# Gate logits kept in their PSUM bank, and the layer norm's epsilon added by a two-operand instruction, in a fused cross-attention and gated self-attention kernel

## The chip, the cores and the metric

The kernel runs on one core of one Trainium2 chip. The metric is the device time of one execution in microseconds; the time before is the median of three runs. A second number, the span, is the stretch of one profiled execution from its first to its last instruction.

## What is computed

Eight sequences of 1024 tokens, 512 channels wide, go through two residual blocks. The first is cross-attention to a context of 1024 by 384 (8 heads of 64), the second self-attention (16 heads of 32) whose output is scaled, token by token, by gates. All is fp32.

```
x = x + tanh(g_xattn) * attn1(layernorm(x), ctx)
x = x + tanh(g_ffn)   * attn2(layernorm(x))

layernorm(x) = (x - mean) / sqrt(var + 1e-5)

# in attn2, per token, on the attention's output h:
gates  = softmax(h @ Wr.T + br)            # 15 routed
routed = gates * top3_mask * 3
sw     = softmax(h @ Ws.T + bs)            # 2 shared
shared = 2 * sw[0] * sw
routed = 2 * sw[1] * routed
out    = h * (shared.sum() + routed.sum())
return out @ Wp.T + bp
```

## The kernel before

The program is one long software pipeline over 16 units called batches here: 0 to 7 are the cross-attention of the eight sequences, 8 to 15 the self-attention of the same eight. Each batch has four groups of heads, each group 16 steps T (two halves of the queries by eight tiles of keys). A step computes scores on TensorE (item `S`, line 920), their exponentials on ScalarE (`ex`, L1122, written to a ring of SBUF buffers), and the weighted values on TensorE (`PV`, L937). The softmax's sums are made on GpSimd, which adds exponential buffers onto one another (`ad`, L812: 128x512, both operands and the result in SBUF, a run of 24 of them per eight steps in the self-attention) before a matmul with ones (`sm`, L949). While one group is attended, the next is projected (`pq`, `pk`, L834), the row maxima of its scores are taken (`mx` on TensorE, L897, and `mxr` on VectorE, L1275), and the next batch is loaded and normed.

A class `Plan` lists every item with its engine, a guessed time, a due step and what it must come after, and simulates the five queues; `Order` turns the result into one fixed order per engine, into semaphore counts, and into the PSUM bank of each unit. The guessed time decides order and banks, not correctness. PSUM's eight banks are one for the weighted values, three for scores, and a ring of four, `aux`, for everything else. A unit holds its bank until the instruction that Order calls its taker counts up `emptied`; the next unit of that bank waits for the count (`wait_emptied`). For the gates' logits the unit is `gt` and the taker `gm`. Every engine works through its list strictly in order.

Two places matter here.

The layer norm of a half batch (items `ln`, `la`, `lb`, `l2`): VectorE takes statistics (L1220, L1223), adds epsilon to four variances (L1225), ScalarE takes logarithm and exponential of them (`la`, L1022 and L1023), VectorE does one Newton step and the bias (`lb`: L1229, L1172, L1173, L1232; all their operands lie in SBUF), and ScalarE norms four tiles (`l2`, L1030), which TensorE transposes (`tr`, L854). There are 32 such halves, named `(batch, half)`.

The gates of a half batch (item `gm`, 16 of them, two per self-attention batch): four tiles of 18 logits lie in one bank of `aux` (L958). VectorE adds the bias and writes the sums to SBUF (L1308), which releases the bank. Everything after works in SBUF: maxima (L1312, L1313), subtractions (L1314, L1315), ScalarE's exponential (L1155), top values and sums (L1318 to L1322), and eight small instructions of 128x4 that combine them into `sc`, the factor per token (L1324 to L1332). `link` marks an instruction whose result the next one reads: VectorE waits for it on its own semaphore. The outputs' evacuation (`ope`, L1340) reads `sc`.

## Time and profile before

| what | us |
|---|---|
| median of 3 runs (5220.41 to 5243.31) | 5229.36 |
| the profiled execution's own time | 5233.06 |
| its span | 5231.3 |
| TensorE busy in the span | 4810.8 (92%) |
| VectorE busy | 3102.1 (59%) |
| ScalarE busy | 2599.0 (50%) |
| GpSimd busy | 3365.1 (64%) |
| mean granted TensorE clock | 0.964 of full |

In the profile a line number stands for the source line of an instruction; where a helper issues it, for the helper's line. "Busy" counts an instruction from its start to its end, also the time in which it has been started and cannot proceed. Idle time in square brackets is that of the engine just before the row, with the instruction that ended it. PE is TensorE, PEld its weight loads, DVE VectorE, ACT ScalarE, POOL GpSimd, SP the queue that issues the DMAs. PEclk is the granted clock as a share of 2.4 GHz; its two levels are 1 and 0.5.

### The profile page before, as it was taken

The page shows a single profiled execution, that of the slowest core. Times are in us where ns is not written, and L with a number is a line of the kernel's source. Part 1 is how long each engine was busy: PE and PEld are TensorE (multiplying, and loading weights), DVE is VectorE, ACT ScalarE, POOL GpSimd, SP SyncE. Part 2 cuts the span into 40 slices and gives each one's busy share as a digit, 9 for nine tenths or more (in the row PEclk, how much of TensorE's full clock was granted, in tenths as well). Part 3 has the DMA queues.
Part 4 walks back from the last instruction along what each step waited for, and adds up shares of the span by engine and source line. Part 5 has one row for each costly group of instructions (what it writes and reads, how often), then busy time and mean ns, then how long its engine had stood idle before and what let it go on. Part 6 is the DMA issues. An engine that isn't in the chain of part 4 may idle for free.

```text
span 5231.3 us, 67135 instructions
## 1 busy us (share of the span) xinstructions
PE 4810.8 (92%) x21696; PEld 2752.7 (53%) x21696; DVE 3102.1 (59%) x3776; ACT 2599.0 (50%) x4673; POOL 3365.1 (64%) x2667
## 2 busy tenths in 40 slices
PE   4999999999999999998998998998998998989998
PEld 3564555555555555564554554554654544645644
DVE  4555555454546464566766757657657666667663
ACT  2444444343434343546646546546456456456364
POOL 1656656564746565637857757667578487478587
PEclk8999999999999999999999999999999999999998
DMA  7353434343343434332233231322222322322320
GB/s 231 93 143 102 121 108 123 111 119 115 93 129 85 137 85 129 90 100 72 53 97 73 55 108 49 81 81 66 75 79 73 89 60 63 89 75 55 97 49 25
DMA packets 285207, 481.08 MB, mean 92 GB/s; under 512 B 32832, under 2 KB 165440, under 8 KB 275648
## 3 DMA queue, kind: packets, MB, share of 16 engines
q1 hardware_dynamic: 284864, 476.79, 33.6%
q8 instruction: 181, 2.97, 0.2%
q14 instruction: 162, 1.33, 0.1%
HBM read 223.14 MB, written 50.33 MB: 52 GB/s over the span
## 4 chain that ended last, share of the span: by engine, by line
PE 48%; DVE 7%; issue 3%; ACT 2%; POOL 1%; SPq 0%; DMA 0%; ACTq 0%; DVEq 0%; POOLq 0%
PE aux L834 14%; PE acc L937 10%; PE aux L897 9%; PE scores L920 9%; DVE nm L1275 4%; PE aux L949 2%; PE aux L958 1%; DVE rs L1225 1%; PE aux L878 1%; POOL added_f L812 1%; PE aux L854 1%; ACT probs L1122 1%; SPq L729 0%; DMA stack<-ck_lo 0%; ACT xs L1030 0%
## 5 line engine op out<-in xcount | busy, mean ns | idle before, releaser
L1275 DVE TENSOR_REDUCE nm<-aux 128x1 f32<-128x1024 f32 x1536 | 1844.1, 1221 | 1208.8 <-PE aux L897 1205.5
L812 POOL TENSOR_TENSOR added<-added,probs 128x512 f32<-128x512 f32 x1433 | 1805.8, 1297 | 966.2 <-PE acc L937 690.8
L1122 ACT ACTIVATE probs<-scores 128x512 f32<-128x512 f32 x2151 | 1190.0, 597 | 915.4 <-PE scores L920 881.2
L920 PE MATMUL scores<-stack 128*128 128x512 f32 x4096 | 1353.0, 420 | 102.2 <-ACT probs L1122 58.8
L897 PE MATMUL aux<-stack 96*128 96x512 f32 (+1 forms) x3072 | 1023.8, 422 | 132.5 <-DVE nm L1275 96.5
L920 PEld LDWEIGHTS scores<-stack 128*128 128x128 f32 x4096 | 740.7, 191 | 716.7 <-issue 276.4
L937 PE MATMUL acc<-probs,vh 128*32 128x512 f32 (+1 forms) x4302 | 979.8, 623 | 62.2 <-ACT vh L1089 37.9
L897 PEld LDWEIGHTS aux<-stack 96*128 96x128 f32 (+1 forms) x3072 | 529.4, 191 | 618.7 <-DVE nm L1275 319.5
L812 POOL TENSOR_TENSOR added_f<-added_f,probs 128x512 f32<-128x512 f32 x537 | 676.8, 1294 | 57.9 <-PE acc L937 35.9
L834 PE MATMUL aux<-xT_hi,wqk 128*128 128x512 f32 x1536 | 580.6, 407 | 14.8 <-ACT qwork L1061 6.9
L1122 ACT ACTIVATE more<-scores 128x512 f32<-128x512 f32 x537 | 300.3, 598 | 176.7 <-PE scores L920 156.7
L834 PEld LDWEIGHTS aux<-xT_hi,wqk 128*128 128x128 f32 x1536 | 290.5, 189 | 113.2 <-issue 47.5
L799 POOL TENSOR_TENSOR cq_lo<-qwork,cq_hi 128x512 fp32r<-128x512 f32 x64 | 82.5, 1289 | 414.4 <-ACT cq_hi L1077 414.4
L937 PEld LDWEIGHTS acc<-probs,vh 128*32 128x32 f32 (+1 forms) x4302 | 158.3, 120 | 346.9 <-issue 240.6
L812 POOL TENSOR_TENSOR added_f<-added_f,more 128x512 f32<-128x512 f32 x231 | 294.4, 1301 | 31.5 <-PE acc L937 25.9
L812 POOL TENSOR_TENSOR added<-added,more 128x512 f32<-128x512 f32 x231 | 291.5, 1293 | 23.5 <-PE acc L937 22.6
L834 PE MATMUL aux<-xT_lo,wqk 128*128 128x512 f32 x768 | 302.7, 394 | 0.0
L937 PE MATMUL acc<-more,vh 128*32 128x512 f32 x1074 | 287.6, 615 | 0.0
L1298 DVE SCALAR_TENSOR_TENSOR aux<-aux,rn 128x512 f32<-128x512 f32 x128 | 88.8, 694 | 251.7 <-ACT rn L1135 236.9
L1122 ACT ACTIVATE added<-scores 128x512 f32<-128x512 f32 x256 | 143.6, 596 | 170.6 <-PE scores L920 167.4
L834 PE MATMUL aux<-wvo,halves_f 128*128 128x512 f32 x768 | 224.0, 435 | 2.9 <-issue 1.5
L818 POOL TENSOR_TENSOR xs<-xs,bo_f 128x512 f32<-128x512 f32 x64 | 81.1, 1288 | 179.5 <-DMA xs<-x_after_xattn 179.5
(129 smaller groups left out, 5106.1 us busy)
## 6 DMA issues: line engine op xcount, KB each, us to landing
wqk<-w_split SPq DMA_DIRECT2D x256, 256.0 KB, 3.8
wvo<-w_split SPq DMA_DIRECT2D x64, 1024.0 KB, 6.9
stack<-cq_hi SPq DMA_DIRECT2D x128, 256.0 KB, 5.0
stack<-ck_hi SPq DMA_DIRECT2D x128, 256.0 KB, 5.0
stack<-cq_hi SPq DMA_DIRECT2D x256, 128.0 KB, 2.3
stack<-ck_hi SPq DMA_DIRECT2D x256, 128.0 KB, 2.4
xs<-in_x SPq DMA_DIRECT2D x16, 1024.0 KB, 6.0
stack<-cq_lo SPq DMA_DIRECT2D x64, 256.0 KB, 4.8
```

What stands on the lines that cost most here:

```text
L799: pool.tensor_tensor(cq["lo"][:, q], qy[:, n], cq["hi"][:, q].bitcast(F32), ALU.subtract).then_inc(qlo_ok, 1)
L812: pool.tensor_tensor(onto, onto, exp_buffer(T, e), ALU.add).then_inc(added_ok, 1)
L818: pool.tensor_tensor(xs[:, t % (TT // 2), :], xs[:, t % (TT // 2), :], bo[:], ALU.add).then_inc(biased, 1)
L834: ins = pe.matmul(out, lhs(a, k), rhs(c, k), start=k == 0 and i == 0, stop=k == whole - 1 and i == 2)
L854: ins = pe.transpose(out[:, i * P:(i + 1) * P], xs[:, i, k * P:(k + 1) * P], ident[:])
L897: ins = pe.matmul(aux[:, b + j, :], stack[used, g % 2, e * ph.SLOTS + qs, t * P:(t + 1) * P], stack[used, g % 2, e * ph.SLOTS + ks, j * HA ...
L920: ins = pe.matmul(scores[:, u % SCORES, :], stack[:, g % 2, e * ph.SLOTS + ks, jt * P:(jt + 1) * P], stack[:, g % 2, e * ph.SLOTS + qs, n ...
L937: ins = pe.matmul(acc[e * D:(e + 1) * D, :], v[:, g, jt * P + e * D:jt * P + (e + 1) * D], exp_buffer(T, e), start=jt == 0, stop=jt == TT - 1)
L949: ins = pe.matmul(out[e * D:(e + 1) * D, :], ones[:, 0:ph.SUM], exp_buffer(T, e), start=i == 0, stop=i == ph.APART)
L1122: act.activation(exp_buffer(T, e), scores[:, (n - 1) % SCORES, :], ACT.Exp, scale=ph.SCALE).then_inc(probs_ok, 1)
L1275: dve.tensor_reduce(nm[:, e * TT + t:e * TT + t + 1], keys, axis=AX.X, op=ALU.max, negate=True).then_inc(emptied["dve"], 1)
L1298: link(dve.scalar_tensor_tensor(src, src, -1.0, rn[:], ALU.mult, ALU.mult))
```

## The change

It has three parts. The layer norm's `var + eps` becomes an instruction that reads the variances twice, `max(var + eps, var)`, which is the same value. The gates' intermediate values are laid out in the same PSUM bank as the logits: sums in place, exponentials from column 256 on, three small vectors at the end of the bank; the maxima, reciprocals and some products stay in SBUF. The bank is released only by the last instruction. The factor `tanh(g_ffn)` is folded into two constants `tg2`, made once at the start by two small instructions, so that each chain has one instruction less (23 instead of 24, counting four per tile group). The planner's guess for `gm` goes from 6 to 5.

```diff
-                    self.add(("gm", 2 * j + half), "dve", 6, b0 + at["out"][half] + 0.5, [("gt", t)])
+                    self.add(("gm", 2 * j + half), "dve", 5, b0 + at["out"][half] + 0.5, [("gt", t)])
...
+        def gate_tiles(bank, first):
+
+            n = TT // 2
+            logits, exps = (bank[:, at:at + n * GC].rearrange("p (t c) -> p t c", c=GC) for at in (first * GC, HALF // 2))
+            return logits, exps, [bank[:, HALF - (i + 1) * n:HALF - i * n] for i in range(3)]
...
-                        act.activation(eg[:, tiles], lg[:], ACT.Exp).then_inc(gates_exp, 1)
+                        act.activation(eg, lg, ACT.Exp).then_inc(gates_exp, 1)
...
+                        dve.tensor_scalar(tg2[:, 0:1], tg[:, 1:2], 2.0, None, ALU.mult)
+                        dve.tensor_scalar(tg2[:, 1:2], tg[:, 1:2], 2.0 * TOPK, None, ALU.mult)
...
-                            dve.tensor_scalar(rs[:, 0, r], mv[:, r, 1], EPS, None, ALU.add).then_inc(rstd_in, 1)
+                            dve.scalar_tensor_tensor(rs[:, 0, r], mv[:, r, 1], EPS, mv[:, r, 1], ALU.add, ALU.max).then_inc(rstd_in, 1)
...
-                        r = slice(first, first + TT // 2)
-                        for t in range(first, first + TT // 2):
-                            ins = dve.tensor_tensor(lg[:, t - first, :], src[:, t * GC:(t + 1) * GC], bg[:], ALU.add)
-                        ins.then_inc(emptied["dve"], 1)
+                        lg, eg, (kept, share, both) = gate_tiles(src, first)
+                        for t in range(TT // 2):
+                            ins = dve.tensor_tensor(lg[:, t, :], lg[:, t, :], bg[:], ALU.add)
+                        link(ins)
+                        dve.tensor_reduce(gm[:, :, 0], lg[:, :, 0:NE], axis=AX.X, op=ALU.max)
+                        link(dve.tensor_reduce(gm[:, :, 1], lg[:, :, SH:SH + 2], axis=AX.X, op=ALU.max))
+                        dve.tensor_tensor(lg[:, :, 0:NE], lg[:, :, 0:NE], gm[:, :, 0:1].to_broadcast([P, TT // 2, NE]), ALU.subtract)
+                        dve.tensor_tensor(lg[:, :, SH:SH + 2], lg[:, :, SH:SH + 2], gm[:, :, 1:2].to_broadcast([P, TT // 2, 2]), ALU.subtract).then_inc(gates_in, 1)
+                        dve.wait_ge(gates_exp, part + 1 - 2 * B)
+                        for t in range(TT // 2):
+                            dve.max(top[:, t, :], eg[:, t, 0:NE])
+                        dve.tensor_reduce(g1[:, 0], eg[:, :, 0:NE], axis=AX.X, op=ALU.add)
+                        link(dve.tensor_reduce(g1[:, 1], eg[:, :, SH:SH + 2], axis=AX.X, op=ALU.add))
+                        link(dve.tensor_reduce(kept, top[:, :, 0:TOPK], axis=AX.X, op=ALU.add))
+                        link(dve.reciprocal(g1[:, 0:2], g1[:, 0:2]))
+
+                        dve.tensor_tensor(g1[:, 2], kept, g1[:, 0], ALU.mult)
+                        dve.tensor_tensor(g1[:, 3], eg[:, :, SH], g1[:, 1], ALU.mult)
+                        link(dve.tensor_tensor(share, eg[:, :, SH + 1], g1[:, 1], ALU.mult))
+
+                        dve.scalar_tensor_tensor(g1[:, 4], share, tg2[:, 1:2], g1[:, 2], ALU.mult, ALU.mult)
+                        link(dve.tensor_tensor(both, share, g1[:, 3], ALU.add))
+                        link(dve.scalar_tensor_tensor(both, both, tg2[:, 0:1], g1[:, 3], ALU.mult, ALU.mult))
+                        dve.tensor_tensor(sc[:, first:first + TT // 2], both, g1[:, 4], ALU.add).then_inc(emptied["dve"], 1)
                         wait_emptied(dve, ("gt", part))
```

The order of all queues stays as it was, with one exception: in the last batch SP issues two stores and two loads alternately that stood in pairs. TensorE's and GpSimd's lists are the same, and every unit of `aux` has the bank that it had. What changes on VectorE is which instructions stand in a chain, and where their operands lie.

VectorE, the end of the gates' chain from the reciprocal on and the two instructions behind it, before (`g` is g1, `L1275` the next row maximum, `L1340` the first output tile's evacuation):

```order
L1322 RECIPROCAL g<-g 128x2x4
L1324 TENSOR_TENSOR g<-g 128x4
L1325 TENSOR_TENSOR sw<-eg,g 128x4
L1326 TENSOR_TENSOR sw<-eg,g 128x4
L1328 TENSOR_TENSOR g<-sw 128x4
L1329 SCALAR_TENSOR_TENSOR g<-g,sw 128x4
L1330 SCALAR_TENSOR_TENSOR g<-g,sw 128x4
L1331 TENSOR_TENSOR g<-g 128x4
L1332 TENSOR_SCALAR sc<-g,tg 128x4
L1275 TENSOR_REDUCE nm<-aux 128x1
L1340 SCALAR_TENSOR_TENSOR xs<-aux,sc,xs 128x512
```

The same place in the changed kernel, whose lines stand a few further down:

```order
L1326 RECIPROCAL g<-g 128x8
L1328 TENSOR_TENSOR g<-aux,g 128x4
L1329 TENSOR_TENSOR g<-aux,g 128x4
L1330 TENSOR_TENSOR aux<-aux,g 128x4
L1332 SCALAR_TENSOR_TENSOR g<-aux,tg,g 128x4
L1333 TENSOR_TENSOR aux<-aux,g 128x4
L1334 SCALAR_TENSOR_TENSOR aux<-aux,tg,g 128x4
L1335 TENSOR_TENSOR sc<-aux,g 128x4
L1281 TENSOR_REDUCE nm<-aux 128x1
L1344 SCALAR_TENSOR_TENSOR xs<-aux,sc,xs 128x512
```

Each of the combining instructions now has one operand in PSUM and one in SBUF, and there is one fewer; what follows them is the same. In the layer norm, before:

```order
L1223 BN_AGGR mv<-st 128x2 x4
L1225 TENSOR_SCALAR rs<-mv 128x4
L1229 TENSOR_TENSOR rs<-rs 128x4
L1172 SCALAR_TENSOR_TENSOR rs<-rs 128x4
L1173 SCALAR_TENSOR_TENSOR rs<-rs 128x4
L1232 SCALAR_TENSOR_TENSOR rs<-mv,rs 128x4
```

and in the changed kernel:

```order
L1229 BN_AGGR mv<-st 128x2 x4
L1231 SCALAR_TENSOR_TENSOR rs<-mv 128x4
L1235 TENSOR_TENSOR rs<-rs 128x4
L1176 SCALAR_TENSOR_TENSOR rs<-rs 128x4
L1177 SCALAR_TENSOR_TENSOR rs<-rs 128x4
L1238 SCALAR_TENSOR_TENSOR rs<-mv,rs 128x4
```

One instruction is of another kind, and the four behind it are untouched.

## Rows read from the trace of the kernel before

**Rows 1.** The page: busy time of each engine.

```profile
PE 4810.8 (92%) x21696; PEld 2752.7 (53%) x21696; DVE 3102.1 (59%) x3776; ACT 2599.0 (50%) x4673; POOL 3365.1 (64%) x2667
```

**Rows 2.** The chain that ended last, VectorE's pieces of L1225, first and last of seven.

```profile
2454.59 8.30 DVE rs L1225
...
4685.99 8.32 DVE rs L1225
```

**Rows 3.** Instructions by line: durations in ns, min/median/max, in all executions of the line.

```profile
L1225 DVE TENSOR_SCALAR rs<-mv x32: 169/1086/8608, 17.1 to 4686.0; 128x4 f32<-128x4 f32 x32
L1232 DVE SCALAR_TENSOR_TENSOR rs<-mv,rs x32: 161/164/1216, 21.1 to 4697.1; 128x4 f32<-128x4 f32 x32
L1325 DVE TENSOR_TENSOR sw<-eg,g x16: 150/156/1330, 2615.2 to 5214.3; 128x4 f32<-128x4 f32 x16
L1299 DVE SCALAR_TENSOR_TENSOR aux<-aux,rn x128: 698/700/700, 172.6 to 5203.1; 128x512 f32<-128x512 f32 x128
L1340 DVE SCALAR_TENSOR_TENSOR xs<-aux,sc,xs x64: 739/750/753, 2625.1 to 5225.9; 128x512 f32<-128x512 f32 x64
```

**Rows 4.** Timeline of (10,1)'s layer norm: start us, us, instruction, [idle before <-releaser].

```profile
2824.53 8.32 DVE L1225 TENSOR_SCALAR rs<-mv 128x4 f32<-128x4 f32 x1
2830.35 2.47 POOL L812 TENSOR_TENSOR added_f<-added_f,probs 128x512 f32<-128x512 f32 x2
2832.76 2.34 DVE L1275 TENSOR_REDUCE nm<-aux 128x1 f32<-128x1024 f32 x2
2833.96 0.77 PE L920 MATMUL scores<-stack 128*128 128x512 f32 x1 [8.26 <-ACT probs L1122]
2835.80 2.93 ACT L1030 ACTIVATE xs<-xs,rs 128x512 f32<-128x512 f32 x4 [1.99 <-DVE rs L1232]
2838.78 1.97 PE L854 MATMUL aux<-ident,xs 128*128 128x128 f32 x8 [3.15 <-ACT xs L1030]
```

**Rows 5.** Timeline of a cross-attention layer norm, (1,1).

```profile
241.26 6.04 DVE L1225 TENSOR_SCALAR rs<-mv 128x4 f32<-128x4 f32 x1
243.68 2.37 POOL L793 TENSOR_TENSOR kv_lo<-raw,kv_hi 128x1024 fp32r<-128x1024 f32 x1
248.31 1.98 PE L937 MATMUL acc<-probs,vh 128*64 128x512 f32 x4 [4.78 <-ACT probs L1122]
248.46 1.16 DVE L1232 SCALAR_TENSOR_TENSOR rs<-mv,rs 128x4 f32<-128x4 f32 x1
249.66 2.93 ACT L1030 ACTIVATE xs<-xs,rs 128x512 f32<-128x512 f32 x4 [0.91 <-DVE rs L1232]
```

**Rows 6.** Timeline of the first gates' chain, batch 8's first half.

```profile
2610.30 0.43 DVE L1308 TENSOR_TENSOR lg<-aux,bg 128x18 f32<-128x18 f32 x4
2615.22 6.18 POOL L812 TENSOR_TENSOR added_f<-added_f,probs 128x512 f32<-128x512 f32 x5
2616.14 1.54 PE L834 MATMUL aux<-wvo,halves_f 128*128 128x512 f32 x6
2622.68 1.19 DVE L1332 TENSOR_SCALAR sc<-g,tg 128x4 f32<-128x4 f32 x1
2625.28 1.19 PE L897 MATMUL aux<-stack 96*128 96x512 f32 x2 [7.60 <-DVE nm L1275]
2626.27 2.77 PE L834 MATMUL aux<-wvo,halves_f 128*128 128x512 f32 x6
```

**Rows 7.** Timeline of the second chain, batch 8's second half.

```profile
2653.80 0.41 DVE L1308 TENSOR_TENSOR lg<-aux,bg 128x18 f32<-128x18 f32 x4
2656.80 0.39 PE L834 MATMUL aux<-xT_hi,wqk 128*128 128x512 f32 x1
2657.25 0.23 DVE L1332 TENSOR_SCALAR sc<-g,tg 128x4 f32<-128x4 f32 x1
```

**Rows 8.** TensorE in 15 us from 6.5 us into seven chains: busy, clock.

```profile
2616.80:2631.80 15.00, 7.40 (x22) 0.66 0.12 42
...
sum 105.00, PE 56.63; mean PE 8.09
```

More of the change, by code:

```diff
@@ L475, in attention @@
         xT_lo = sb("xT_lo", [P, NG, N], F32R)
-        qwork, more, bv, bo_f, blk, wg, lg, eg, top = earlier(
+        qwork, more, bv, bo_f, blk, wg, top = earlier(
             ("qwork", [P, 3, 2, HALF], F32), ("more", [P, F.NP - X.NP, HALF], F32), ("bv", [P, DM], F32), ("bo_f", [P, DM], F32),
-            ("blk", [P, P], F32), ("wg", [P, NG, GC], F32), ("lg", [P, TT // 2, GC], F32), ("eg", [P, TT, GC], F32),
-            ("top", [P, TT, 8], F32))
+            ("blk", [P, P], F32), ("wg", [P, NG, GC], F32), ("top", [P, TT // 2, 8], F32))
         halves_f, = earlier(("halves_f", [P, 3, 2, NG, P], F32R))
@@ L511, in attention @@
         bg = sb("bg", [P, GC])
-        gm = sb("gm", [P, TT, 2])
-        g1 = sb("g1", [P, 4, TT])
-        sw = sb("sw", [P, TT, 2])
+        gm = sb("gm", [P, TT // 2, 2])
+        g1 = sb("g1", [P, 5, TT // 2])
+        tg2 = sb("tg2", [P, 2])
         sc = sb("sc", [P, TT])
@@ L1151, in _ @@
                     elif kind == "gm":
-                        first = it[1] % 2 * TT // 2
-                        tiles = slice(first, first + TT // 2)
+                        lg, eg, _ = gate_tiles(aux[:, o.bank["gt", it[1]], :], it[1] % 2 * TT // 2)
                         act.wait_ge(gates_in, it[1] + 1 - 2 * B)
-                        act.activation(eg[:, tiles], lg[:], ACT.Exp).then_inc(gates_exp, 1)
+                        act.activation(eg, lg, ACT.Exp).then_inc(gates_exp, 1)
             @block.vector
@@ L1305, in _ @@
                         first = part % 2 * TT // 2
-                        r = slice(first, first + TT // 2)
-                        for t in range(first, first + TT // 2):
-                            ins = dve.tensor_tensor(lg[:, t - first, :], src[:, t * GC:(t + 1) * GC], bg[:], ALU.add)
-                        ins.then_inc(emptied["dve"], 1)
-                        wait_emptied(dve, ("gt", part))
-                        dve.tensor_reduce(gm[:, r, 0], lg[:, :, 0:NE], axis=AX.X, op=ALU.max)
@@ L1313, in _ @@
-                        link(dve.tensor_reduce(gm[:, r, 1], lg[:, :, SH:SH + 2], axis=AX.X, op=ALU.max))
-                        dve.tensor_tensor(lg[:, :, 0:NE], lg[:, :, 0:NE], gm[:, r, 0:1].to_broadcast([P, TT // 2, NE]), ALU.subtract)
-                        dve.tensor_tensor(lg[:, :, SH:SH + 2], lg[:, :, SH:SH + 2], gm[:, r, 1:2].to_broadcast([P, TT // 2, 2]), ALU.subtract).then_inc(gates_in, 1)
-                        dve.wait_ge(gates_exp, part + 1 - 2 * B)
-                        for t in range(first, first + TT // 2):
-                            dve.max(top[:, t, :], eg[:, t, 0:NE])
@@ L1319, in _ @@
-                        dve.tensor_reduce(g1[:, 0, r], eg[:, r, 0:NE], axis=AX.X, op=ALU.add)
-                        link(dve.tensor_reduce(g1[:, 1, r], eg[:, r, SH:SH + 2], axis=AX.X, op=ALU.add))
-                        link(dve.tensor_reduce(g1[:, 2, r], top[:, r, 0:TOPK], axis=AX.X, op=ALU.add))
-                        link(dve.reciprocal(g1[:, 0:2, r], g1[:, 0:2, r]))
-                        dve.tensor_tensor(g1[:, 2, r], g1[:, 2, r], g1[:, 0, r], ALU.mult)
-                        dve.tensor_tensor(sw[:, r, 0], eg[:, r, SH], g1[:, 1, r], ALU.mult)
@@ L1326, in _ @@
-                        link(dve.tensor_tensor(sw[:, r, 1], eg[:, r, SH + 1], g1[:, 1, r], ALU.mult))
-                        link(dve.tensor_tensor(g1[:, 3, r], sw[:, r, 0], sw[:, r, 1], ALU.add))
-                        dve.scalar_tensor_tensor(g1[:, 0, r], g1[:, 3, r], 2.0, sw[:, r, 0], ALU.mult, ALU.mult)
-                        link(dve.scalar_tensor_tensor(g1[:, 1, r], g1[:, 2, r], 2.0 * TOPK, sw[:, r, 1], ALU.mult, ALU.mult))
-                        link(dve.tensor_tensor(g1[:, 0, r], g1[:, 0, r], g1[:, 1, r], ALU.add))
@@ L1332, in _ @@
-                        link(dve.tensor_scalar(sc[:, r], g1[:, 0, r], tg[:, 1:2], None, ALU.mult))
+                        lg, eg, (kept, share, both) = gate_tiles(src, first)
[4 more added lines that the diff above has]
+                        link(dve.tensor_reduce(gm[:, :, 1], lg[:, :, SH:SH + 2], axis=AX.X, op=ALU.max))
```

## The prediction, made before the changed kernel was run

> **What bounds the kernel now.** I read the page first: TensorE is busy 92% of the span, VectorE 59%, GpSimd 64% [rows 1]. TensorE is the bound, and VectorE's time costs something only where TensorE stands still for it. The chain that ended last says where: L1225, which adds epsilon to four numbers per partition, is on it seven times with 8.30 to 8.6 us [rows 2]. The durations by line show what is wrong with it: 169 ns at best, 8608 at worst [rows 3]. Then the timelines, for whom each stall delays.
>
> In the layer norm of (10,1), L1225 starts at 2824.53 and ends at 2832.85, just when GpSimd's unbroken run of additions ends (2830.35 + 2.47 = 2832.82) [rows 4]. ScalarE waits for it and all exponentials behind, so TensorE is idle for 8.26 us, then 3.15 more until ScalarE has normed [rows 4]. The same stretch returns in batches 9 to 15. The second halves of batches 1 to 7 are the milder form: 6.04 us in L1225, 4.78 us of TensorE [rows 5].
>
> The gates' first chain starts at 2610.30 and ends at 2623.87, the second one, with GpSimd silent, from 2653.80 to 2657.48: 13.6 against 3.7 us for the same 24 instructions [rows 6, 7]. The small products of SBUF operands take 150 ns or up to 1330, about one addition of GpSimd (1.24 us: 6.18 / 5) [rows 3, 6]. The next row maximum stands behind them, and TensorE waits 7.60 us for it [rows 6]. In seven windows of 15 us, each beginning 6.5 us into such a chain, TensorE is busy 56.63 of 105 us: 48.4 us are idle [rows 8]. The eighth first-half chain lies in the tail.
>
> So two kinds of wait: a two-input SBUF instruction waits for GpSimd's running addition, L1225 in these places for the whole run. One with an operand in PSUM does not wait: L1299 (bank and SBUF in, bank out) took 698 to 700 ns all 128 times [rows 3].
>
> **The change, part by part.**
>
> *Gates.* All waiting instructions of the chain get a PSUM operand, so I take 3.7 us everywhere, as quiet [rows 7], the one instruction saved (0.16) against the slightly longer links. In the first halves the row maximum then comes 9.9 us earlier, and the 48.4 us of TensorE's idle time go. GpSimd covers none of it: its run ends at 2625.1 either way, and the sum matmul that needs it stands well behind the output products. The clock gives more. In the stall the granted clock falls to 1.2 GHz, 0.66 of full on average over the first window [rows 8], and the six matmuls behind it take 2.77 us where the six before took 1.54 [rows 6]. In the first case TensorE works at the low level from 2625.28 to about 2631 and loses half of that, 2.7 us (the half-speed matmuls [rows 6]); I take 2.4 each, a little less as two of the seven stalls are shorter, 17 in all. Bounds: 0 (the clock falls anyway) and 2.7 x 7 = 19.
>
> The new wait: the bank is held 3.7 us instead of 0.4. In the second half its next user is the projection, 3.00 us behind the chain's start [rows 7]: 0.7 us late, and the other cases I looked at start later than that, so 0.7 in all. In the first half it is the second output tile, 5.84 us behind (some 4.4 once ScalarE's exponential is no longer late) [rows 6]: covered. If the cover went, each chain would cost what it is longer than that. Tail: the output's evacuation comes earlier, but the run of additions ends where it did; 2 us, between 0 and 5.
>
> The Trainium skill (VectorE: DVE Perf Modes, the TRN2 errata) gives 120 cycles fixed for a PSUM source against 58 for an SBUF source, estimated 65 ns more per instruction, 1.5 us more per chain of 23. By it the second halves would wait 2.2 us in the worst case and the sum would lose about 4 us. No row here shows the difference for such small shapes.
>
> *Layer norm.* The new instruction has two inputs in SBUF and no PSUM operand. L1232 is of this kind, and 1.16 us is what it took while GpSimd went on [rows 5]; 1.22 is the worst of 32 [rows 3]. So it waits for one addition. But then the four instructions of `lb` come while GpSimd's run still goes on, where now they come after it. For (10,1), additions end each 1.24 us back from 2832.82: 2825.4, 26.6, 27.9, 29.1, 30.3, 31.6. Epsilon is done at 2825.5, the two row maxima take 2.34 [rows 4], the first of `lb` gets the end at 27.9 or just misses it, and the last ends at 31.6 or 32.8. ScalarE's L1030 starts at 31.7 to 33.0 instead of 35.80: 2.8 to 4.1 us, so 3.5 x 7 = 24.5. Had the four ended as quietly as now, it would be 7.4 each, the outer bound. The low clock behind stays, as TensorE still idles 8 us.
>
> In (1,1) epsilon is ready at 242.4, but `lb` has to pass the additions' ends at 243.7, 246.05 (the long L793 [rows 5]), 247.3 and, with two exponentials earlier, 248.5. L1030 starts at 248.6 instead of 249.66: 1.1 us x 7 = 8. Bounds 0 and the 4.78 of TensorE, 33 us.
>
> The Trainium skill (SBUF — State Buffer, Who interferes with whom) says that a VectorE instruction in a two-port mode, which the old form can enter, or with two SBUF inputs (the new form) waits for the running GpSimd instruction only. For the new form the rows agree (1.22 at most); for the old one they do not, with 8.3 us over seven additions. By the page's rule the old wait would be as short as the new one; that is part of rival 1.
>
> *Rest.* Two 128x1 instructions at the start, 0.16 us each beside the loading: nothing. The two SP rows in the tail: nothing. ScalarE's exponential of the gates between banks: a quarter of a microsecond as before.
>
> **Sum.** 48.4 + 17 - 0.7 + 2 for the gates, 24.5 + 8 for the norm: 99 us from the profiled execution's 5233.1, which is 4 above the median: 5134.
>
> **The rivals.**
> 1. *The norm gains nothing*, because the new instruction waits for the whole run too, or because something else than the instruction's form held the old one. For: same place, same SBUF tiles, and 169 ns where GpSimd was silent says nothing on the form. Against: L1232, with two SBUF inputs, never took over 1.22 [rows 3]. Without the 32 us of the norm it is 5233 - 67 = 5166. Chance 0.10. The rule of the page SBUF — State Buffer in the Trainium skill (only the running instruction is waited for) ends here too.
> 2. *The gates' stall turns into a wait for GpSimd.* TensorE arrives 8 to 10 us earlier where additions still run, and ring buffers are freed only by them. For: GpSimd has no gap from 2615 to 2625 [rows 6]. Against: the first exponentials behind the stall reuse buffers added before 2617, and the next ones need none. Losing four fifths of the 48 us: 5173. Chance 0.11.
> 3. *The chain does not stop waiting.* The two instructions with `tg2` read it and g1 from SBUF; if that counts as two inputs, 2.2 us of 9.9 stay per chain, with the clock's share some 17 us: 5151. Against: L1340 has the same kinds of operands (bank, `sc` as a scalar from SBUF, a tile in SBUF) and stays between 739 and 753 ns in 64 executions [rows 3]. Chance 0.06.
> 4. *Slower: the bank held.* If in-place work in PSUM waits as SBUF work did, each of the 14 chains holds its bank c us, and TensorE waits c - 4.4 and c - 4 for it. The 99 us are eaten when 14c - 59 = 99, at c = 11.3, half a microsecond per instruction. At today's 13.6 it is 5134 + 132 = 5266. L1299's 700 ns speak against it [rows 3]. Chance 0.02.
>
> **How the numbers follow.** The forecast has 0.71. Beyond the sum the norm may give 4 more (4.1 each) and 17 if the low clock behind it goes too, the cross-attention 25, the tail 3; I let the low end hold 39 of these 49: 5095. The high end takes in rivals 1 to 3, each alone, with 7 us more for a norm at its lower bounds or a run like the slowest of the three shown: 5180. Half a percent, 26 us, is about what a measurement here can tell from no change. Only rival 4, and a mixture of 1, 2 and a clock that falls elsewhere, end within or above it: faster 0.95, same 0.03, slower 0.02.
>
> **What would show it.** The epsilon instruction's maximum at 1.2 us and its name gone from the chain; the four of `lb` in batches 9 to 15 up from 0.16 to 1.2; first-half chains of 3.7 us and no 7.6 us wait of L897; GpSimd's runs ending where they did; a short wait for a bank at the first projection matmul behind second-half chains; low clock gone behind the gates, present behind the norm. Wrong would be: an epsilon instruction above 2.5 us, chains above 5 us, or new waits of exponentials for GpSimd.

## The result, and the profile after

The changed kernel takes 5191.9 us, the median of five executions (5164.6 to 5201.0), against 5229.4 (5220.4 to 5243.3) for the kernel before: ratio 0.9919, with a 95% interval of 0.9901 to 0.9938. It is 37 us faster. The forecast was 5134 and the range 5095 to 5180, so the direction was right and the size was not: about 60 of the 99 us did not come. The profiled execution took 5195.9 us. Its busy times stand against [rows 1]:

```profile
span 5194.1 us, 67121 instructions
PE 4795.6 (92%) x21696; PEld 2744.4 (53%) x21696; DVE 3068.5 (59%) x3762; ACT 2597.6 (50%) x4673; POOL 3366.2 (65%) x2667
```

Of the 37.2 us by which the span shrank, 15.2 are TensorE busy for less time (4810.8 to 4795.6), the other 22 are idle time that went.

**The norm gained nothing.** The durations by line (ns, min/median/max) answer to [rows 3]; L1231 is the epsilon instruction, L1297 the subtraction `hsl` that splits the attention's output, L1329 and L1332 (with `tg2`) are in the gates' chain:

```profile
L1231 DVE SCALAR_TENSOR_TENSOR rs<-mv x32: 161/1200/8595, 17.0 to 4651.8; 128x4 f32<-128x4 f32 x32
L1297 DVE TENSOR_TENSOR halves_f<-vh,halves_f x64: 669/682/9970, 2597.9 to 5182.4; 128x512 fp32r<-128x512 f32 x64
L1329 DVE TENSOR_TENSOR g<-aux,g x16: 151/152/154, 2612.9 to 5175.5; 128x4 f32<-128x4 f32 x16
L1332 DVE SCALAR_TENSOR_TENSOR g<-aux,tg,g x16: 221/222/225, 2613.2 to 5175.8; 128x4 f32<-128x4 f32 x16
```

The new form's maximum is 8595 ns where the old one's was 8608. The timeline of (10,1)'s norm is that of [rows 4] with another opcode: 8.32 us, until GpSimd's run of additions ends (2819.75 + 2.47 = 2822.22), and TensorE idle for 8.24 us, then for 3.16:

```profile
2813.92 8.32 DVE L1231 SCALAR_TENSOR_TENSOR rs<-mv 128x4 f32<-128x4 f32 x1
2819.75 2.47 POOL L817 TENSOR_TENSOR added_f<-added_f,probs 128x512 f32<-128x512 f32 x2
2823.34 0.77 PE L925 MATMUL scores<-stack 128*128 128x512 f32 x1 [8.24 <-ACT probs L1127]
2828.18 1.11 PE L859 MATMUL aux<-ident,xs 128*128 128x128 f32 x4 [3.16 <-ACT xs L1035]
```

**The chain is quiet in all 16 places**, 3.56 to 3.58 us each where it was 10.8 to 13.8 in the first halves. But a new wait stands right behind it. The timeline of batch 9's first half, and the subtraction of batch 10's:

```profile
2969.91 0.43 DVE L1314 TENSOR_TENSOR aux<-aux,bg 128x18 f32<-128x18 f32 x4
2973.32 0.16 DVE L1335 TENSOR_TENSOR sc<-aux,g 128x4 f32<-128x4 f32 x1
2974.66 0.74 DVE L1344 SCALAR_TENSOR_TENSOR xs<-aux,sc,xs 128x512 f32<-128x512 f32 x1
2975.32 9.96 DVE L1297 TENSOR_TENSOR halves_f<-vh,halves_f 128x512 fp32r<-128x512 f32 x1
2979.81 4.92 POOL L817 TENSOR_TENSOR added_f<-added_f,probs 128x512 f32<-128x512 f32 x4
2985.20 1.21 DVE L1281 TENSOR_REDUCE nm<-aux 128x1 f32<-128x1024 f32 x1
2986.56 1.19 PE L902 MATMUL aux<-stack 96*128 96x512 f32 x2 [7.55 <-DVE nm L1281]
...
3344.06 1.39 DVE L1297 TENSOR_TENSOR halves_f<-vh,halves_f 128x512 fp32r<-128x512 f32 x1
```

The chain ends at 2973.48. Then the subtraction of two SBUF tiles takes 9.96 us, to 0.55 us behind the end of GpSimd's run (it needs 0.67 by itself), the row maximum is late again, and TensorE waits 7.55 us for it: nearly the 7.60 of [rows 6], from another instruction. In batch 10 the same subtraction waits for one addition only, 1.39 us. An instruction that waits to the end of GpSimd's run is called held from here on. L1297 was held in four of the seven windows that answer to [rows 8], each beginning 6.8 us into a chain (TensorE's busy us, then the granted clock as a share of full speed):

```profile
2617.20:2632.20 15.00, 14.94 (x80) 1.00 0.66 174
2976.70:2991.70 15.00, 7.45 (x25) 0.77 0.18 55
3345.50:3360.50 15.00, 14.90 (x79) 1.00 0.69 179
3707.10:3722.10 15.00, 14.88 (x79) 1.00 0.64 168
4069.30:4084.30 15.00, 7.45 (x28) 0.77 0.20 55
4441.60:4456.60 15.00, 7.45 (x28) 0.77 0.19 55
4816.00:4831.00 15.00, 7.45 (x24) 0.77 0.18 55
sum 105.00, PE 74.52; mean PE 10.65
```

Idle time in them fell from 48.4 us to 105 - 74.52 = 30.5, so 17.9 us came and 4 x 7.55 = 30.2 stayed. What one batch gains shows in the distance between successive second-half norms; in batch 8 L1297 is not held, in batch 9 it is:

```profile
2453.55 8.33 DVE L1231 SCALAR_TENSOR_TENSOR rs<-mv 128x4 f32<-128x4 f32 x1
...
3183.02 8.30 DVE L1231 SCALAR_TENSOR_TENSOR rs<-mv 128x4 f32<-128x4 f32 x1
```

With 2813.92 between them that is 360.4 us for batch 8 and 369.1 for batch 9, where before it was 369.9 [rows 2, 4] and 370.6. The three batches in which L1297 is not held gain 9.6, 12.9 and 9.9 us, about the prediction's (48.4 + 17) / 7 = 9.3 each; batches 9, 12 and 13, in which it is held, gain 1.5, -0.9 and 0.2.

### The profile page after: what moved, and what is told of

Same layout as the page of the kernel before. It is cut to its first block, busy times and chain, and to the rows that moved or that the text cites. A ratio compares the mean times of both kernels' runs of the same rounds, so it can differ in the third digit from the quotient of the medians.

```text
span 5194.1 us, 67121 instructions
## 1 busy us (share of the span) xinstructions
PE 4795.6 (92%) x21696; PEld 2744.4 (53%) x21696; DVE 3068.5 (59%) x3762; ACT 2597.6 (50%) x4673; POOL 3366.2 (65%) x2667
## 4 chain that ended last, share of the span: by engine, by line
PE 48%; DVE 6%; issue 4%; ACT 2%; POOL 1%; SPq 1%; DMA 0%; ACTq 0%; POOLq 0%; DVEq 0%
PE aux L839 15%; PE acc L942 10%; PE aux L902 9%; PE scores L925 8%; DVE nm L1281 3%; PE aux L954 2%; PE aux L963 1%; DVE rs L1231 1%; PE aux L883 1%; POOL added_f L817 1%; PE aux L859 1%; SPq L734 1%; ACT probs L1127 0%; DMA stack<-ck_lo 0%; ACT xs L1035 0%
## 5 line engine op out<-in xcount | busy, mean ns | idle before, releaser
L817 POOL TENSOR_TENSOR added<-added,more 128x512 f32<-128x512 f32 x231 | 291.2, 1290 | 24.3 <-PE acc L942 23.7
L823 POOL TENSOR_TENSOR xs<-xs,bo_x 128x512 f32<-128x512 f32 x64 | 81.8, 1292 | 163.2 <-DMA xs<-in_x 163.1
```

What stands on the lines that cost most here:

```text
L817: pool.tensor_tensor(onto, onto, exp_buffer(T, e), ALU.add).then_inc(added_ok, 1)
L823: pool.tensor_tensor(xs[:, t % (TT // 2), :], xs[:, t % (TT // 2), :], bo[:], ALU.add).then_inc(biased, 1)
```

## The experiments

All ratios are to the kernel before, from runs on the same chip. Expectations are quoted as they were written before each run.

**1. The two parts alone.** e1 is the changed kernel with the old epsilon instruction:

```diff
-dve.scalar_tensor_tensor(rs[:, 0, r], mv[:, r, 1], EPS, mv[:, r, 1], ALU.add, ALU.max)
+dve.tensor_scalar(rs[:, 0, r], mv[:, r, 1], EPS, None, ALU.add)
```

> The changed kernel with the old epsilon instruction (one SBUF tile and a constant). Theory A (the new form of the epsilon instruction does nothing, the whole gain is the gates'): same time as the changed kernel, 5165 to 5201, L1231 again at some 8.6 us at most, and batches 9 to 15 with 8.2 us of idle TensorE in the second half's norm. Theory B (the norm did gain and the gates less): 20 to 30 us slower than the changed kernel, some 5220. In both the subtraction L1297 behind the gates' first-half chain should wait some 10 us in about half of the seven ffn batches, since the epsilon instruction stands 200 us away from it.

Measured: 5180.3 us, ratio 0.9906 (0.9892 to 0.9919). e2 is the kernel before with the opposite edit:

> The kernel before with the new epsilon instruction alone (the variance's column twice, from SBUF). Theory A: no change, ratio 0.998 to 1.002, the instruction up to 8.6 us. Theory B (what the prediction had): the instruction at 1.2 us at most, 32 us faster, ratio 0.994.

Measured: 5229.0 us, ratio 0.9995 (0.9986 to 1.0004). Theory A holds on both sides: the norm's edit is worth nothing, the gates' edit all of the gain. The rows of the epsilon instruction, e1's and e2's:

```profile
L1231 DVE TENSOR_SCALAR rs<-mv x32: 170/1151/8606, 17.2 to 4640.9; 128x4 f32<-128x4 f32 x32
...
L1225 DVE SCALAR_TENSOR_TENSOR rs<-mv x32: 161/1186/8593, 17.0 to 4678.0; 128x4 f32<-128x4 f32 x32
```

L1297 was held in two of the seven windows of e1 (4.4 and 6.0 us of TensorE) against four in the profiled run of the changed kernel. Whether it is held is close to a toss. The executions of the changed kernel spread over 36 us, the five of before beside them over 23, and the 15 of before beside e1 and e2 over 12.

**2. Another form for epsilon.** e3 adds epsilon by a reduction:

```diff
-mv = sb("mv", [P, TT, 2])
+mv = sb("mv", [P, TT, 3])
...
+link(dve.memset(mv[:, :, 2], EPS))
...
-dve.scalar_tensor_tensor(rs[:, 0, r], mv[:, r, 1], EPS, mv[:, r, 1], ALU.add, ALU.max)
+dve.tensor_reduce(rs[:, 0, r], mv[:, r, 1:3], axis=AX.X, op=ALU.add)
```

> The changed kernel, epsilon added by a tensor_reduce over the variance and a third column that holds epsilon, so one SBUF input and the kind of instruction that took 0.17 to 0.22 us within GpSimd's runs. Theory C (what waits for the end of a run is set by the place: the first instruction there that cannot run beside an addition, whatever its form): epsilon 0.2 us, the first instruction of lb (the product of two SBUF tiles) then takes some 6 to 8 us in batches 9 to 15, and the time stays at 5165 to 5201. Theory D (only this one instruction is unlucky): epsilon 0.2 us, each of lb's four waits for one addition at most, 25 to 33 us faster than the changed kernel.

Measured: 5185.4 us, ratio 0.9912 (0.9899 to 0.9926), as the changed kernel. The rows of L1232 (the reduction) and L1236 (first of `lb`), and the timeline of (10,1):

```profile
L1232 DVE TENSOR_REDUCE rs<-mv x32: 160/161/165, 17.1 to 4652.4; 128x4 f32<-128x8 f32 x32
L1236 DVE TENSOR_TENSOR rs<-rs x32: 150/824/7846, 20.4 to 4654.7; 128x4 f32<-128x4 f32 x32
...
2832.04 0.16 DVE L1232 TENSOR_REDUCE rs<-mv 128x4 f32<-128x8 f32 x1
2834.39 5.99 DVE L1236 TENSOR_TENSOR rs<-rs 128x4 f32<-128x4 f32 x1
2837.85 2.50 POOL L817 TENSOR_TENSOR added_f<-added_f,probs 128x512 f32<-128x512 f32 x2
2840.41 0.16 DVE L1176 SCALAR_TENSOR_TENSOR rs<-rs 128x4 f32<-128x4 f32 x1
```

Theory C: the reduction passes, and the next instruction that cannot pass waits for the same end of the run (2840.35). The place decides, not the instruction.

**3. Pauses in GpSimd.** In the traces one addition starts some 40 ns before the one ahead has ended. e4 makes GpSimd wait, before each addition, for its own last one:

```diff
+if ph.adds(T, e) > 1:
+    pool.wait_ge(added_ok, ph.adds(T, e) - 1)
 pool.tensor_tensor(onto, onto, exp_buffer(T, e), ALU.add).then_inc(added_ok, 1)
```

> The changed kernel, and GpSimd waits before each addition of probabilities until its own previous one has ended (a semaphore it gets from itself), so that additions no longer overlap end to start. Theory C (VectorE's instruction waits for a moment in which no addition is in progress, and back to back additions leave none): with some 0.1 us between additions the instruction gets in at the next boundary, epsilon at most 1.4 us, L1297 at most 2 us, the 8.24 us of idle TensorE in the norm of batches 9 to 15 down to 4 to 5, and GpSimd's runs 5 to 10% longer; 30 to 90 us faster than the changed kernel, unless TensorE then waits for additions. Rival (the wait has nothing to do with overlap, the run's work has to be done first): the waits stay at 8 us or more, and the time gets 0 to 30 us longer.

Measured: 5160.4 us, ratio 0.9860 (0.9845 to 0.9876), 31 us faster than the changed kernel. The long waits are gone:

```profile
L1233 DVE SCALAR_TENSOR_TENSOR rs<-mv x32: 161/194/1417, 17.0 to 4606.4; 128x4 f32<-128x4 f32 x32
L1299 DVE TENSOR_TENSOR halves_f<-vh,halves_f x64: 670/681/1759, 2559.6 to 5147.9; 128x512 fp32r<-128x512 f32 x64
L956 PE MATMUL aux<-added,ones 128*64 128x512 f32 (+1 forms) x512 | 105.2, 624 | 21.2 <-POOL added L819 21.0
```

But an addition now comes each 1.45 us instead of 1.24, and TensorE's sum matmul L956 waited 21 us for GpSimd (last row: busy us, mean ns, idle us and its releaser; in the changed kernel it was 2.3). With the sums that read `added_f` it waited 54 us, against 8 in the changed kernel. e7 puts the same pauses into the kernel before:

> The kernel before with GpSimd's pause before every addition, so without the change. Theory C: the epsilon instruction's waits shrink from up to 8.6 to 1.4 us as in the changed kernel, the gates' chain still waits for one addition some eight times, a little longer each as additions come every 1.45 us: some 30 us faster than the kernel before as on the changed kernel (5192 to 5160), so 5195 to 5205. If the chain's waits shrink too (a pause is open to several short instructions in a row), 5170 to 5185.

Measured: 5164.7 us, ratio 0.9877 (0.9860 to 0.9893). The last case came closest, 5 us below its range: the old chain shrank from 13.6 us to 6.8 to 7.9, as two short instructions get through one pause.

**4. What makes a wait long.** Four kernels computed nothing of the model: GpSimd does runs of additions, and VectorE, busy with row maxima out of PSUM that disturb nobody, puts a probe into each.

> No part of the model is computed: GpSimd does runs of 16 additions of 128x512, and VectorE puts one probe into each, behind one or seven row maxima of 1024 elements out of PSUM and one more of 64 to 1024 elements (steps of 67 ns, so that the probe meets every part of an addition). Probes: the new epsilon instruction (two SBUF inputs, 4 wide), the old one (one), the reduction, and a subtraction of two tiles 512 wide. Theory C (VectorE needs a moment without an addition): the reduction 0.16 us always; the three others wait for one addition or for the whole rest of the run (up to some 16 us), and phase or depth within the run decides which. Theory of one addition (as the prediction had it): no wait above 1.3 us. If the form decides, one4 and two4 differ.

In runs of 16 additions every probe waited for the end of one addition, at most 1.30 us (1.82 for the 512 wide one, which needs 0.69 by itself), whatever its form or phase; the reduction never waited:

```profile
L86 DVE SCALAR_TENSOR_TENSOR rs<-mv x32: 164/664/1297, 13.7 to 636.3; 128x4 f32<-128x4 f32 x32
L88 DVE TENSOR_SCALAR rs<-mv x32: 170/670/1302, 647.6 to 1270.2; 128x4 f32<-128x4 f32 x32
L90 DVE TENSOR_REDUCE rs<-mv x32: 160/161/163, 1281.4 to 1904.0; 128x4 f32<-128x8 f32 x32
```

One input or two makes no difference. The deepest probe there stood 10 us into its run. m2 went deeper:

> No part of the model is computed: runs of 26 additions, a probe 5, 12 or 16 row maxima deep in each; half the runs with two waits before each addition (both satisfied), as the kernel has them, half with one; half with the probe followed by three row maxima that are ready, half with nothing behind it until it has ended. Probes: the old epsilon instruction, the 4 wide product of lb, the subtraction 512 wide. In the first such measurement no probe passed more than two boundaries. If age of the run, the second wait or the ready instructions behind it make the wait last until the run's end, that group alone shows waits of 10 to 20 us; if none does, all stay under 1.35 us (1.9 for the subtraction) and the cause is in what the other engines do.

It is the age of GpSimd's run. The 72 probes up to 7.6 us into it all waited for one addition. Of the 72 between 15.2 and 16.0 us, 25 waited for one (the last at 15.75) and 47 to the end of the run, up to 17 us; the 72 beyond 20 us all waited to the end. The number of waits ahead of an addition made no difference (with one, 14 of the 36 at the border waited for one addition only, with two, 11). What stood behind the probe made none that these numbers show (16 of 36 with nothing behind it, 9 of 36 with maxima). Two neighbours, 15.7 and 15.8 us into their runs of 31.76 us:

```profile
300.91 31.76 POOL L65 TENSOR_TENSOR added<-added,probs 128x512 f32<-128x512 f32 x26 [0.30 <-DVE nm L82]
316.58 0.26 DVE L90 TENSOR_SCALAR rs<-mv 128x4 f32<-128x4 f32 x1
332.98 31.76 POOL L65 TENSOR_TENSOR added<-added,probs 128x512 f32<-128x512 f32 x26 [0.30 <-DVE nm L82]
348.79 15.97 DVE L90 TENSOR_SCALAR rs<-mv 128x4 f32<-128x4 f32 x1
```

The kernel's traces fit. In those of before, the change, e1 and e2, of 56 epsilon instructions in second halves, all 15.8 us or more behind GpSimd's last gap, 55 took 5.8 to 8.6 us; of 31 in first halves within a run, 3.6 us or less behind the gap, none took over 1.4. m3 asks what makes the run young again:

> No part of the model is computed: runs of 26 additions, probes 8, 11, 14 and 18 row maxima deep, in four kinds of run: plain; with a 4 wide product of VectorE after the 5th or after the 9th maximum, which is let in at the next boundary; with one gap in GpSimd before its 6th addition. Theory T (a clock of some 15.5 us that starts anew at a gap of GpSimd and whenever VectorE is let in): plain runs wait long from depth 12 on, so at 14 and 18; with the early product or the gap at 5 (some 7 us in) depth 14 waits one addition only and depth 18 long or at the border; with the product at 9 all four wait one addition only. Rival (only the age of GpSimd's run counts): the early product changes nothing, the gap does. Second rival (only VectorE's own last turn counts): the gap changes nothing.

The gap does, the single product does not. In plain runs the border was at 18.2 us. With the product 6 or 11 us in, probes up to 16 us in waited for one addition and those from 18.8 us in all waited to the end, though VectorE had had its turn as little as 6.6 us before. With the gap, of 0.08 us and 6 us into the run, all probes up to 18.5 us got in at the next boundary, and so did eight of the ten at 22.7 to 23.5 us, some 17 behind the gap. The rival "only GpSimd's run counts" held for a lone narrow turn. m4 then tried turns in quick succession:

> No part of the model is computed: runs of 26 additions of GpSimd, and a 4 wide product of VectorE as the probe, behind (a) 10 to 18 row maxima and nothing else, (b) nine maxima and then one to five pairs of product and maximum, (c) nine maxima and 2 to 10 products back to back, (d) four maxima, two subtractions 512 wide back to back, and 5 to 11 maxima. (a) gives the border again, 15 to 18 us. Theory U (turns in quick succession keep VectorE's turn open): (c) one addition each up to the last at some 24 us, (b) too or longer waits at its end. Rival (only GpSimd's run counts): beyond the border of (a) all wait to the run's end, in (b) and (c) already at the product that crosses it. (d) tells whether an addition drawn out to 2.4 us by VectorE counts as a gap: then its 11 maxima, at some 20 us, still wait for one addition only.

Plain runs gave the border again between 18.2 and 18.4 us. Products back to back, or 2.4 us apart, from 11 us on kept every wait at one addition, up to 24 us into the run, with at most 3.5 us from one turn to the next. Two 512 wide subtractions 5 to 8 us in had the same effect up to 23.3 us. The rows are a plain probe 18.2 and one 18.4 us into the run, and ten products in a row with the probe behind them at 24.3:

```profile
574.89 0.17 DVE L93 TENSOR_TENSOR rs<-rs 128x4 f32<-128x4 f32 x1
607.49 13.37 DVE L93 TENSOR_TENSOR rs<-rs 128x4 f32<-128x4 f32 x1
...
2553.73 12.03 DVE L88 TENSOR_TENSOR st<-st 128x4 f32<-128x4 f32 x10
2566.88 1.31 DVE L93 TENSOR_TENSOR rs<-rs 128x4 f32<-128x4 f32 x1
```

This fits the old chain, in which it was not tested by itself. In batch 8 of before VectorE's last wide subtraction ended at 2604.2, the chain's first SBUF turn came at 2611.1, and the others followed at most 2.7 us from each other, each paying one addition and keeping the way open for the next one; the subtraction behind it, at 2625.7, found the run at its end. By taking long, the old chain had led it past. In the seven windows the chain's first turn stood 17.3 to 18.9 us into the run and 6.8 to 8.4 us behind the last subtraction, and was never held. The new chain takes no turn at all, so that in batch 9 the subtraction is the first for some 12 us, 22 us into the run. In such places, 21.9 to 25.1 us into the run and 11.5 to 14.6 us behind the last turn, it was held 14 times of 28 (the changed kernel 4 of 7, e1 2, e3 4, and e9 below 4). The epsilon instructions of the second halves, over 100 us behind the last turn, were held 55 times of 56.

**5. Pauses only where they are needed.** e5 puts the pause only before additions that the order places from 10 items ahead to 30 items behind an `ln`, an `lb` or an `hsl`, 201 of 832 groups of additions:

```diff
+near = [i for i, it in enumerate(sched) if it[0] in ("ln", "lb", "hsl")]
+paused = {it for i, it in enumerate(sched) if it[0] == "ad" and any(-10 <= i - v <= 30 for v in near)}
...
+if it in paused and ph.adds(T, e) > 1:
+    pool.wait_ge(added_ok, ph.adds(T, e) - 1)
```

> The changed kernel with GpSimd's pause only before those additions that the order puts near a layer norm or near the subtraction that splits the output (201 of 832 groups of them). Theory C: the long waits of L1231 and L1297 (8 to 10 us) go as with pauses everywhere, while TensorE and ScalarE wait less for additions (with pauses everywhere the sum matmul waited 21 us for them): 5125 to 5150. If the windows miss the places: like the changed kernel.

Measured: 5059.9 us, ratio 0.9674 (0.9660 to 0.9688), 132 us faster than the changed kernel and 65 below the range expected. Its page and the same rows:

```profile
PE 4771.7 (94%) x21696; PEld 2735.0 (54%) x21696; DVE 2947.2 (58%) x3762; ACT 2600.2 (51%) x4673; POOL 3377.7 (67%) x2667
L1235 DVE SCALAR_TENSOR_TENSOR rs<-mv x32: 161/165/1379, 17.0 to 4534.4; 128x4 f32<-128x4 f32 x32
L1301 DVE TENSOR_TENSOR halves_f<-vh,halves_f x64: 680/688/1770, 2545.5 to 5048.1; 128x512 fp32r<-128x512 f32 x64
L958 PE MATMUL aux<-added,ones 128*64 128x512 f32 (+1 forms) x512 | 103.4, 612 | 0.2 <-POOL added L821 0.2
```

Against the changed kernel, TensorE is idle for 110 us less (5194.1 - 4795.6 = 398.5 to 288.1) and busy for 24 us less. In the 18 us around each norm the idle time falls from 85 to 41 us over the seven second halves of batches 9 to 15, from 34 to 14 over those of batches 1 to 8, and from 55 to 41 over the first halves of batches 1 to 15; the four waits behind the gates (30 us) are gone: 44 + 20 + 14 + 30 = 108. e6 adds the reduction of e3 on top:

> The same with epsilon added by the reduction, which waits for no addition: one wait less of up to 1.3 us in each of 14 norms, but where lb's own waits follow it is eaten. 0 to 10 us faster than the one without: 5120 to 5150.

Measured: 5053.2 us, ratio 0.9665 (0.9651 to 0.9679): the fastest of all, by less than the intervals separate, and like e5 far below the range expected. e8 takes the change away and keeps the windows:

> The kernel before, without the change, with the same pauses in the same windows. What the change is worth once the long waits are gone: the gates' first-half chain should last some 7 us as with pauses everywhere (6.8 to 7.9) against 3.57 in the changed kernel with windows, so some 3.3 us x 8 with the clock's share behind it: 25 to 45 us slower than the changed kernel with windows, 5085 to 5105. If the windows miss the chain, it stays at 13.6 us and the time is 5120 to 5140.

Measured: 5067.1 us, ratio 0.9688 (0.9675 to 0.9702). The chain lasts 6.8 to 7.9 us as expected, but TensorE waited only 2.18 us behind it in batch 9. With the long waits gone the whole change is worth 7 us between the medians, not the 25 to 45 expected, and the intervals of the two ratios overlap: it may be worth nothing. In the profiled executions TensorE is idle for 15 us less with the change (303.6 to 288.1) and busy for 11 us more (4761.1 to 4771.7). e9 has pauses near the norms only:

> The changed kernel with pauses near the layer norms only, none near the subtraction behind the gates. Tells the two waits apart. If L1297's 10 us waits in some of the seven ffn batches cost TensorE 7.5 us each and the low clock behind (4 of 7 in the profiled run of the changed kernel), this is 25 to 60 us slower than with both windows (5085 to 5120); if those waits were cheap and the norm made the whole difference, 5060 to 5070.

Measured: 5091.3 us (5078.6 to 5098.8), ratio 0.9735 (0.9719 to 0.9751). L1301 was held 6.9 to 10.0 us four times, and TensorE waited 25.5 us for it in all. The profiled execution's span is 25.4 us longer than e5's, the median 31: the held subtractions cost 6 to 8 us each.

**6. One pause in 8 or 16.** The condition is now `ph.adds(T, e) % 8 == 0`, or 16.

> The changed kernel with GpSimd's pause before every 8th addition, some 10 us apart, everywhere. Theory T: no wait longer than one addition is left though 7 of 8 additions still follow without a gap, and there are fewer pauses than in the windows: 5045 to 5065. If each instruction needs a pause of its own close by, waits of up to 8 additions stay: 5100 to 5190.

> The same with every 16th addition, some 20 us apart. Theory T: 20 us is more than the 15.5, so part of the long waits stays, by where the pauses happen to fall: 5070 to 5150, slower than with every 8th. If a gap anywhere in the run is enough: as with every 8th.

Measured: 5112.7 (ratio 0.9775, 0.9760 to 0.9789) and 5147.9 us (0.9851, 0.9838 to 0.9865). The epsilon instruction and the third of `lb`, of e10; then the epsilon instruction of e11:

```profile
L1233 DVE SCALAR_TENSOR_TENSOR rs<-mv x32: 161/170/1422, 16.9 to 4586.6; 128x4 f32<-128x4 f32 x32
L1179 DVE SCALAR_TENSOR_TENSOR rs<-rs x32: 161/1184/1217, 20.9 to 4590.5; 128x4 f32<-128x4 f32 x32
...
L1233 DVE SCALAR_TENSOR_TENSOR rs<-mv x32: 161/687/7583, 17.0 to 4614.7; 128x4 f32<-128x4 f32 x32
```

A gap each 10 us removes every long wait (no wait over two additions, 2.3 us, is left), one each 20 us does not, as the border of 15 to 18 us has it. But e10 missed its 5045 to 5065 by some 50 us: the last three of `lb`'s four instructions still wait for an addition each. A second-half norm of batches 9 to 15 costs TensorE 7.6 us against 5.8 with pauses before every addition near it (and 12.2 in the changed kernel). Those seven norms are 13 of the 54 us between the spans of e10 and e5; the second halves of batches 1 to 8 are 8, the first halves 14, and TensorE's busy time 15.

**7. Turns given back to the chain.** e12 puts three narrow SBUF products that nothing uses into the new chain:

```diff
 link(dve.reciprocal(g1[:, 0:2], g1[:, 0:2]))
+link(dve.tensor_tensor(spare[:, 0], g1[:, 0], g1[:, 1], ALU.mult))
...
```

> The changed kernel with three products of SBUF tiles, 4 wide, that nothing uses, put into the gates' chain behind the reciprocal, behind the product of the share and near the end, so that the chain waits for three additions again and VectorE has turns shortly ahead of the subtraction L1297 behind it. Theory U: that subtraction no longer waits beyond one addition, the chain lasts 6 to 7.5 us, and TensorE's 7.5 us stall in some batches is gone: 5160 to 5180, against 5165 to 5201 of the changed kernel. Rival: the subtraction waits for the run's end as before or more often, since it comes later in the run: 5190 to 5215.

Measured: 5212.5 us (5185.7 to 5240.9), ratio 0.9972 (0.9954 to 0.9990), inside the rival's range, but for another reason. Behind the chain the subtraction never waited beyond one addition, as Theory U says (1164 ns at most), but only in three of the eight first halves did GpSimd's run still go on there. In the other five the first spare product, 2.5 us into the chain, was itself held to the run's end:

```profile
2985.16 0.43 DVE L1315 TENSOR_TENSOR aux<-aux,bg 128x18 f32<-128x18 f32 x4
2987.62 12.27 DVE L1328 TENSOR_TENSOR spare<-g 128x4 f32<-128x4 f32 x1
3001.57 0.77 PE L840 MATMUL aux<-wvo,halves_f 128*128 128x512 f32 x1 [11.69 <-DVE sc L1339]
```

Whichever instruction takes the first turn after a long time is the one that may be held.

## Why the prediction was right in direction and wrong in size

- **Gates, 48.4 us.** Right as a mechanism for the chain, and in the three windows where L1297 was not held it came in full. The step that failed is "In the first halves the row maximum then comes 9.9 us earlier, and the 48.4 us of TensorE's idle time go": I followed TensorE's row maximum past the chain but not the SBUF subtraction that stands between the chain and the next one. It waited in four of seven windows and kept 30.2 of the 48.4.
- **Clock, 17 us.** The size for one stall was about right, but only three of the seven went. In the three batches without one TensorE's busy time fell by 2.3 us on average (-0.5, 3.5 and 4.0), near the 2.4 taken for each; in batches 9, 12 and 13 by 0.7. That the whole span's busy time fell by 15.2 is partly luck: 3.4 of it lie ahead of batch 9's second norm, where no gates are, and 2.8 in batch 14 and the tail. The granted clock is 1.00, so 2.4 GHz, in the windows without a stall and 0.77 in those with one; in the seven windows of before it was 0.66 or 0.77.
- **The held bank, -0.7.** Zero. In the 12 us from the start of each second-half chain of batches 8 to 14 TensorE has no gap above 0.2 us. The Trainium skill (VectorE: DVE Perf Modes, the TRN2 errata) gives fixed costs from which I had estimated 65 ns more for each PSUM operand; the product L1329 took 151 ns at least with one where L1325 before took 150 [rows 3], and the whole chain 3.57 us against 3.69 with one instruction more. No such price shows at these widths.
- **Norm, 24.5 + 8 us.** Nothing came. This is rival 1, at 5166 with a chance of 0.10. The step that failed is "L1232 is of this kind, and 1.16 us is what it took while GpSimd went on", and from it "So it waits for one addition". The epsilon instruction took up to 8595 ns where that gave 1.2 us. L1232 always ran right behind others of its kind or behind the run's end; it never took the first turn late in a run. I read a property of the instruction out of rows that showed a property of the place. The rival's own words, "something else than the instruction's form held the old one", were the cause. Rival 1 was also believed to leave the gates' 67 us whole, so even it gave 26 us too much.
- **Rivals 2 to 4.** The exponentials into `probs` and `more` waited 33 us for GpSimd in all, 25 before: 8 us, not rival 2's 39. The instructions with `tg2` do not wait (L1332 took 221 to 225 ns in all 16 places). The bank held costs nothing.
- **The chances.** Two faults with one root were counted as apart: both parts rested on the belief that a two-input SBUF instruction waits for one addition only.
- **The base.** The sum is taken from the profiled execution's 5233.1; from the median, which is what is compared, it would give 5130. This changes nothing above.

The Trainium skill (SBUF — State Buffer, Who interferes with whom) says that of a VectorE instruction with two SBUF inputs, or in a two-port mode, and a GpSimd instruction the second waits for the first only. The trace agrees while GpSimd's run is younger than some 15 us, or VectorE has just had its turns; beyond that the waits went over some 5 to 14 additions. The two kinds, the old form (which can enter a two-port mode) and the new one (two SBUF inputs), waited alike (m1, e1, e2).

**What stays open.** Why the border lay at 15.2 to 15.8 us in m2 and at 18.2 in m3 and m4. Their plain runs are written alike, but in the traces the overlap of one addition with the next grows from 43 to 73 ns through a run of m2 and stays at 42 in m3 and m4; no run tells whether that moves the border, and in the kernels the overlap at L1297 is 31 to 49 ns whether it is held or not. Open too is why L1297, some 12 us behind VectorE's last turns, is held in one batch and not in the next, and what in the hardware counts. The runs show when a wait becomes long, not by which circuit.

## What to carry to other kernels

An instruction that "sometimes takes 8 us instead of 0.16" should be read by its place: compare it with its neighbours by how long the other engine has been working without a gap, before its form is changed. When short waits are taken out of a chain, look at the next instruction that needs the same thing: the waits may have been what kept its way open. Where GpSimd works in runs of more than some 12 such additions beside VectorE, a wait on its own last result near the places that matter is cheap (0.2 us each) and here (e8, 161 us) was worth four times the change. Before every addition it was not cheap: TensorE then waited 54 us for the sums (e4).

## What the runs showed of the hardware that I had not expected

- Beside 128x512 additions of GpSimd that follow each other without a gap, a VectorE instruction on SBUF operands waits for at most one of them (1.30 us in the probes, 1.37 in the kernels) early in the run, and to the end of the run (up to 17 us) from 15 to 18 us on, if VectorE had no such turn shortly before. With its last turns 11.5 to 14.6 us back (L1297) it was held 14 times of 28.
- A gap of GpSimd of 0.17 us in the kernel and 0.08 in m3, from a wait on its own last addition, ends this; a lone narrow turn of VectorE, 6.6 us before, does not; in m4 a row of turns at most 3.5 us apart did, and so did two wide ones 5 to 8 us into the run.
- A reduction of SBUF data (0.16 us, 32 times of 32 in e3) and narrow instructions with an operand in PSUM (0.15 to 0.23 us) were never held, in the oldest runs too.
- In e7 two short SBUF instructions in a row pass around one gap (0.15 to 0.16 us each), and the third waits for the next.
